# Second pass of a gated cross-attention kernel: the masks are written into the score banks by VectorE and ScalarE instead of by TensorE

## The chip, the cores and the metric

The kernel runs on one NeuronCore of one Trainium2 chip. The metric is the device time of one execution in microseconds (us), smaller is better. Engines: TensorE (PE, its weight loads PEld), VectorE (DVE), ScalarE (ACT), GpSimd (POOL) and SyncE (SP), which only issues DMAs here.

## The reference

```python
# x: (128, 128, 256); ctx_1024: (128, 128, 256); mask: (128, 128, 128) int32, per item [query, key]
# block 0: attention without weights (16 heads of 16), then an fp8 GEMM, each added to x through tanh(gate)
# block 1:
qh, kh, vh = (proj(q, Wq, bq), proj(k, Wk, bk), proj(v, Wv, bv))
scores = einsum('bhqd,bhkd->bhqk', qh, kh) / sqrt(16)
scores = where(mask[:, None] == 0, -1e9, scores)
attn = softmax(scores, axis=-1)
ctx = einsum('bhqk,bhkd->bqhd', attn, vh)
out = concat @ Wo.T + bo            # added to x through tanh(g_xattn[1])
# then a layer norm, an int8-like activation quantisation with one scale for the whole tensor, a ternary GEMM
```

There are 128 batch items, and each item is one tile of 128 queries by 128 keys by 256 features. The change concerns only the masked attention of block 1.

## The kernel before

X stays in SBUF for all 128 items. The program runs three passes over it: the first (`step_a`) is block 0, the second (`step_b`) is the attention of block 1 with the statistics of its last norm, the third (`step_c`) is the quantised GEMM. Every engine has its own written-out order; there is no scheduler. In the second pass a step i works on several items at once: `live(off)` says whether item i + off exists, the projections are those of item i+1, the maximum scores those of item i, the exponent scores those of item i-2, the normalising and output projection those of item i-3, and a norm's last part those of item i-7. Fori loops repeat eight written-out steps. Steps alternate between even and odd k; in even steps ScalarE makes two normalised inputs `xn`, in odd ones GpSimd works out the norm statistics of a pair.

Softmax takes its row maxima from one set of scores (queries on the partitions, `max_pair`, two PSUM banks, `bank_max`) and its exponentials from a second, transposed set (keys on the partitions, `exp_pair`, two banks, `bank_exp`). Each bank pair holds half of the 16 heads at a time, so a step fills each pair twice: `fill(0, ...)` and `fill(1, ...)`. A fill of the maximum pair is read by one VectorE reduction (`max_pair_of`, L787), one of the exponent pair by one ScalarE exponential (`exp_pair_of`, L553). `U` and `UM` are the projected queries and keys, `UM` with the even or the odd heads set to zero; GpSimd makes `UM` (L519, L521) and reports it with `m_made`.

In `fill`, the matmuls of a 32-partition row group r are L1044 (maximum) and L1051 (exponent); the two kinds use different row groups and run side by side. The mask is added by TensorE: L1035 writes the mask into the maximum banks through an identity ahead of the scores (2 matmuls of 512 columns), L1058 adds the transposed mask to the exponent banks behind them (2 more). L1039 writes the negated row maxima (`sh_T`), which VectorE splits into two bf16 parts (`sh`), TensorE transposes (L1157) and ScalarE copies out (L612).

The further orders that the change's steps meet:

- TensorE: fill 0, L1026 (attention output back), L1157, L1165 and L1173 (projections q, k and v), fill 1, L1068 (weighing with V, pair 1), L1192, wait for `m_made` and `xn_made`, L1206 (transposes of the next inputs), L1068 (pair 0), L1218 (output projection).
- ScalarE: L553 (exponential 1), L612, in even steps L557 twice (`xn`), L625 (`n2`, held in the tile `ff_y`), L630 (V), L553 (exponential 0), L638, L645, L547.
- GpSimd: in odd steps the statistics L485 to L502, L505, then wait for `n2_made`: L510 and L512 (gamma and beta on `n2`), then L519 and L521 (`UM`).
- VectorE: L886, norm statistics, L916, L787, L927 and L778, L934 (mask to bf16, 0 or -2^100), L941 (`U`), L787, L948 and L950 (`sh`).

Of the kernel before, what the change touches and what calls it, by code (L numbers as in the profile page):

```python
# [30 lines left out]
P = 128  # L31
# [24 lines left out]
def build(nc, x, ctx, mask, g_xattn, g_ffn, f8_kernel, in_scale, kernel_scale, f8_bias,  # L56
# [12 lines left out]
    with stack:  # L69
# [46 lines left out]
        sh_T = [sb(f"sh_T{n}", [P, 4 * P], BF16)[:, :] for n in range(2)]  # L116
# [109 lines left out]

        bv_made = sem("bv_made")
# [305 lines left out]
        def _(act):  # L533
# [70 lines left out]

            def step_b(i, k, live):
# [27 lines left out]
                if live(-2):  # L633
                    exp_pair_of(0)
                if live(-3):
# [3 lines left out]
                      .then_inc(cn_out, 1)  # L639
                if live(2):  # L640
# [31 lines left out]
        def _(vec):  # L672
# [205 lines left out]

            def step_b(i, k, live):
# [13 lines left out]
                if live(5):  # L893
                    n_bn = mine(v.bn_stats(st6_b[n][:, 0:6], xs(i + 5)))
                if odd and (live(5) or live(-5)) and (live(1) or live(-9)):
# [16 lines left out]
                if live(-8):  # L912
# [5 lines left out]
                    if live(-7 + 1):  # L918
# [3 lines left out]
                if live(0):  # L922
                    max_pair_of(0, k % 2).then_inc(max_read, 1)
                if live(-3):
                    vec.wait_ge(attn_back, 1)
                    vec.sem_inc(attn_back, -1)
                    mine(v.reciprocal(rden[:, :], bank_oh[:, :, DH]))  # L927
                    settle()
                    attn_normed().then_inc(attn_read, 1)
                if live(1):  # L930

                    vec.wait_ge(mask_in[(k + 1) % 2], 16)
                    vec.sem_inc(mask_in[(k + 1) % 2], -16)
                    n_m = mine(v.tensor_scalar(mask_b[(k + 1) % RING], mask_i[(k + 1) % 2], 0.0, MASKED,  # L934
                                               ALU.is_equal, ALU.mult))
                    vec.wait_ge(qk_proj, 1)
                    vec.sem_inc(qk_proj, -1)  # L937
                    settle(n_m)
                    if live(3):
                        vec.sem_inc(mask_used, 1)  # L940
                    v.tensor_tensor(U[(k + 1) % RING][:, :, :], bank_t[0][:, :].rearrange("p (c t) -> p c t", c=4),  # L941
# [328 lines left out]
```

## Time and profile before

| | before |
|---|---|
| median of 3 runs | 2464.26 us (2459.34 to 2464.36) |
| the profiled execution | 2460.99 us, its span 2459.2 us |
| mean granted TensorE clock | 0.978 |
| busy: PE, PEld | 2168.4 us (88%), 1537.5 us (63%) |
| busy: DVE, ACT, POOL | 1611.5 us (66%), 1430.5 us (58%), 1129.2 us (46%) |
| second pass | from about 892 to about 2345 us of the span |

Busy times are summed records of an engine, and a record can overlap the next one. In the rows of the timeline a line is one instruction or several of the same kind in a row ("x2"), with the start in us from the span's start and the duration in us; what stands in brackets is the idle time of the engine just before it and what ended it. `PEq L1149` is a wait of the TensorE's instruction queue at line 1149.

### The profile page before, as it was taken

To read this page: it belongs to the slowest core of one execution; us is meant where nothing else is said; L and a number is where in the kernel's file an instruction comes from. 1 tells how busy PE (TensorE), PEld (TensorE's weight loads), DVE (VectorE), ACT (ScalarE), POOL (GpSimd) and SP (SyncE) were. 2 spreads that over 40 slices of the span, in tenths; PEclk is the share of its full clock that TensorE was granted. 3 is DMA by queue.
4 is the path that set the end of the run, shared out by engine and by line. 5 is a ranking of instruction groups with operands and counts; after the bars stand their busy time and mean duration, and the time that the engine had idled before them with its cause. 6 is when DMAs were issued, how large, how long until landed. Compare 5 with 4: busy or idle time off the path is not lost. (4 is left out here: it accounts for less than half of the span.)

```text
span 2459.2 us, 74014 instructions
## 1 busy us (share of the span) xinstructions
PE 2168.4 (88%) x25884; PEld 1537.5 (63%) x25884; DVE 1611.5 (66%) x3702; ACT 1430.5 (58%) x2375; POOL 1129.2 (46%) x1905
## 2 busy tenths in 40 slices
PE   3888888888888859999999999999999999999957
PEld 2666666666666547667666766666666666666635
DVE  4888888888888845555555555555554555555569
ACT  1788787887877734444444444544544444544469
POOL 2666666666666633433343343434333433434320
PEclk6999999999999979999999999999999999999989
DMA  2111111111111000000000000000000000000025
GB/s 70 45 40 43 40 41 43 40 41 42 39 43 43 15 21 21 21 18 21 18 21 18 19 20 18 21 18 21 17 21 18 21 18 18 21 18 21 4 85 189
DMA packets 95564, 80.56 MB, mean 33 GB/s; under 512 B 11392, under 2 KB 95360, under 8 KB 95360
## 3 DMA queue, kind: packets, MB, share of 16 engines
q1 hardware_dynamic: 95360, 77.44, 10.4%
q8 instruction: 176, 2.88, 0.5%
q14 instruction: 28, 0.23, 0.0%
HBM read 60.63 MB, written 16.78 MB: 31 GB/s over the span
## 5 line engine op out<-in xcount | busy, mean ns | idle before, releaser
L553 ACT ACTIVATE probs<-bank_exp 128x1024 f32<-128x1024 f32 x512 | 523.8, 1023 | 679.0 <-ACTq L552 679.0
L787 DVE TENSOR_REDUCE a_nmax<-bank_max 128x8 f32<-128x1024 f32 x512 | 625.7, 1222 | 330.9 <-DVEq L786 326.2
L1044 PE MATMUL bank_max<-UM,U 32*128 32x256 f32 x4096 | 588.7, 405 | 4.6 <-PEq L1079 2.5
L1051 PE MATMUL bank_exp<-UM,U 32*128 32x256 f32 x4096 | 531.1, 377 | 0.0
L510 POOL TENSOR_TENSOR ff_y<-ff_y,gamma_bc 128x256 f32<-128x256 f32 x128 | 92.8, 725 | 804.8 <-POOLq L509 804.8
L1068 PE MATMUL bank_o<-probs,V 128*17 128x128 f32 x8192 | 324.2, 275 | 127.4 <-PEq L1064 126.9
L1051 PEld LDWEIGHTS bank_exp<-UM,U 32*128 32x128 f32 x4096 | 391.9, 185 | 0.6
L1068 PEld LDWEIGHTS bank_o<-probs,V 128*17 128x17 f32 x8192 | 187.7, 96 | 275.7 <-issue 275.3
L1044 PEld LDWEIGHTS bank_max<-UM,U 32*128 32x128 f32 x4096 | 354.3, 186 | 8.6 <-issue 7.9
L1165 PE MATMUL bank_t<-spare,wT 128*128 128x128 f32 x2048 | 259.1, 280 | 0.9 <-PEq L1162 0.9
L1165 PEld LDWEIGHTS bank_t<-spare,wT 128*128 128x128 f32 x2048 | 241.3, 194 | 1.6 <-issue 1.6
L886 DVE SCALAR_TENSOR_TENSOR X<-bank_m,gate,X 128x256 f32 (+1 forms) x128 | 61.9, 484 | 269.1 <-DVEq L885 269.1
L1039 PE MATMUL bank_exp<-sh_T,ones_b 32*128 32x512 bf16 x1024 | 199.7, 385 | 16.1 <-PEq L1115 11.3
L547 ACT ACTIVATE attn_T<-bank_o 128x512 f32<-128x512 f32 x256 | 152.9, 597 | 90.6 <-ACTq L546 90.4
L1035 PE MATMUL bank_max<-ff_qT,ident 128*128 128x512 bf16 x512 | 152.8, 380 | 34.0 <-PEq L1149 33.5
L941 DVE TENSOR_TENSOR U<-bank_t,bqk_T 128x512 f32<-128x512 f32 x128 | 88.5, 691 | 133.9 <-DVEq L937 133.9
L1026 PE MATMUL bank_o<-identf,attn_T 128*128 128x128 f32 x1024 | 162.9, 282 | 0.9 <-PEq L1024 0.9
L1026 PEld LDWEIGHTS bank_o<-identf,attn_T 128*128 128x128 f32 x1024 | 119.5, 142 | 69.3 <-issue 45.9
L1039 PEld LDWEIGHTS bank_exp<-sh_T,ones_b 32*128 32x128 bf16 x1024 | 50.4, 91 | 175.2 <-issue 151.4
L1058 PE MATMUL bank_exp<-ident,ff_qT 128*128 128x512 bf16 x512 | 157.1, 389 | 0.0
L472 POOL TENSOR_TENSOR spare<-spare 128x512 f32<-128x512 f32 x64 | 81.5, 1273 | 144.0 <-POOLq L471 87.0
L449 POOL TENSOR_SCALAR UM<-U,heads_eo 128x512 f32<-128x512 f32 x128 | 119.4, 933 | 59.9 <-POOLq L448 59.8
(163 smaller groups left out, 4151.6 us busy)
## 6 DMA issues: line engine op xcount, KB each, us to landing
ctx<-in_ctx SPq DMA_DIRECT2D x256, 128.0 KB, 2.1
X<-in_x SPq DMA_DIRECT2D x128, 128.0 KB, 2.1
out_y<-X SPq DMA_DIRECT2D x64, 256.0 KB, 2.1
ff_qq<-in_mask_BxSxS_ik SPq DMA_DIRECT2D x128, 64.0 KB, 1.8
X<-in_L_xattn_Wq SPq DMA_DIRECT2D x1, 256.0 KB, 2.7
X<-in_L_xattn_Wk SPq DMA_DIRECT2D x1, 256.0 KB, 3.1
X<-in_L_xattn_Wv SPq DMA_DIRECT2D x1, 256.0 KB, 3.8
X<-in_L_xattn_Wo SPq DMA_DIRECT2D x1, 256.0 KB, 4.2
```

What stands on the lines that cost most here:

```text
L449: mine(nc.gpsimd.tensor_scalar(UM[s][:, :, 0, :], U[s][:, :, :], heads_eo[:, 0:1], 0.0, ALU.mult, ALU.add))
L547: nc.scalar.activation(attn_T[:, :, :].rearrange("p g t -> p (g t)"), bank_o[:, :], ACT.Copy)\
L553: nc.scalar.activation(a_probs[n], exp_pair[:, :, :, :].rearrange("p i h t -> p (i h) t"), ACT.Exp, scale=SCALE).then_inc(probs_made, 1)
L787: return v.tensor_reduce(a_nmax[:, k2, n * H // 2:(n + 1) * H // 2], max_pair[:, :, :, :].rearrange("p i h t -> p (i h) t"), axis=AX.X, op ...
L1026: last = nc.tensor.transpose(bank_o[:, g * P:(g + 1) * P], attn_T[:, g, :], identf[:, :])
L1035: mm(max_pair[:, b, :, :], ident[:, :], mask_now.rearrange("p (o t) -> p o t", o=1) .broadcast_to([P, HG, P]), start=True, stop=False, ski ...
L1039: mm(exp_pair[:, r % 2, :, :], ones_b[32 * r:32 * r + 32, :], sh_T[ring][32 * r:32 * r + 32, :], start=True, stop=False, skip_group_check= ...
L1044: last = mm(max_pair[:, r % 2, 2 * c:2 * c + 2, :], U[now][32 * r:32 * r + 32, c, :], UM[now][32 * r:32 * r + 32, DC + c, :, :], start=not ...
L1051: last = mm(exp_pair[:, r % 2, 2 * c:2 * c + 2, :], U[before][32 * r:32 * r + 32, DC + c, :], UM[before][32 * r:32 * r + 32, c, :, :], sta ...
L1058: last = mm(exp_pair[:, b, :, :], mask_before, ident[:, :].rearrange("p (o t) -> p o t", o=1) .broadcast_to([P, HG, P]), start=False, stop ...
L1068: last = mm(bank_o[32 * j:32 * j + VW, (2 * c + n) * P:(2 * c + n + 1) * P], V[k4][:, 8 * c + 2 * r + e, :], a_probs[n][:, r % 2 * HG + 2 ...
L1165: last = mm(bank_t[0][:, n * P:(n + 1) * P], wT[n // DC][:, c, n % DC * P:(n % DC + 1) * P], in_T[(k + 1) % 2][:, n // DC * DC + c, :], st ...
```

## The change

TensorE no longer writes masks. VectorE copies the mask (`mask_b`, queries on the partitions) into both maximum banks, spread over 8 heads, directly after each maximum reduction (`seed_max`). ScalarE copies the transposed mask into both exponent banks in the same way after each exponential (`seed_exp`). All score matmuls and the shift now add to what is there (`start=False`). Once, at the start of the second pass, TensorE writes to all four banks so that later matmuls add. The transposed mask comes from a fifth transpose beside the four of `sh`, and the copy L612 takes five blocks instead of four. In `fill` the shift moves from the first to the last place. On VectorE, the reduction of fill 0 and what follows it move ahead of the norm's aggregates and L916.

```diff
+        sh_mask_T = [sb(f"sh_T{n}", [P, 5 * P], BF16)[:, :] for n in range(2)]
+        sh_T = [t[:, 0:4 * P] for t in sh_mask_T]
+        mask_T = [t[:, 4 * P:5 * P] for t in sh_mask_T]
...
         # scalar
+            def seed_exp(ring):
+                nc.scalar.activation(exp_pair[:, :, :, :].rearrange("p i h t -> p (i h) t"),
+                                     mask_T[ring].rearrange("p (o t) -> p o t", o=1).broadcast_to([P, H // 2, P]),
+                                     ACT.Copy).then_inc(exp_seeded, 1)
+            def exp_settled(n):
+                act.wait_ge(scores, 1)
+                act.sem_inc(scores, -1)
+                nc.scalar.activation(a_probs[n], exp_pair[:, :, :, :].rearrange("p i h t -> p (i h) t"), ACT.Exp,
+                                     scale=SCALE).then_inc(act_own, 1)
+            def probs_settled():
+                act.wait_ge(act_own, 1)
+                act.sem_inc(act_own, -1)
+                act.sem_inc(probs_made, 1)
...
                 if live(-2):
-                    exp_pair_of(1)
+                    exp_settled(1)
                 if live(-1):
                     act.wait_ge(shift_Td, 1)
                     act.sem_inc(shift_Td, -1)
-                    nc.scalar.activation(sh_T[(k + 1) % 2], bank_tb[1][:, 0:4 * P], ACT.Copy).then_inc(shift_out, 1)
+                    nc.scalar.activation(sh_mask_T[(k + 1) % 2], bank_tb[1][:, 0:5 * P], ACT.Copy).then_inc(shift_out, 1)
+                if live(-2):
+                    probs_settled()
+                    seed_exp(k % 2)
...
                 if live(-2):
-                    exp_pair_of(0)
+                    exp_settled(0)
                 if live(-3):
                     act.wait_ge(cn_T, 1)
...
+                if live(-1):
+                    if live(-2):
+                        probs_settled()
...
+                    seed_exp((k + 1) % 2)
...
         # vector
+            def seed_max(ring):
+                v.tensor_copy(max_pair[:, :, :, :].rearrange("p i h t -> p (i h) t"),
+                              mask_b[ring].rearrange("p (o t) -> p o t", o=1).broadcast_to([P, H // 2, P]))\
+                 .then_inc(max_seeded, 1)
...
+                if live(0):
+                    n_max = mine(max_pair_of(0, k % 2))
+                    settle(n_max)
+                    seed_max(k % RING)
...
                 if live(0):
                     n_max = mine(max_pair_of(1, k % 2))
                     settle(n_max)
-                    vec.sem_inc(max_read, 1)
+                if live(1):
+                    seed_max((k + 1) % RING)
...
         # tensor, in fill
-                if now is not None and masked:
-                    for b in range(2):
-                        mm(max_pair[:, b, :, :], ident[:, :], mask_now.rearrange("p (o t) -> p o t", o=1)
-                           .broadcast_to([P, HG, P]), start=True, stop=False, skip_group_check=True)
...
-                                      start=not masked, stop=True, skip_group_check=True)
+                                      start=not seeded, stop=True, skip_group_check=True)
...
-                if before is not None and masked:
-                    for b in range(2):
-                        last = mm(exp_pair[:, b, :, :], mask_before, ident[:, :].rearrange("p (o t) -> p o t", o=1)
-                                  .broadcast_to([P, HG, P]), start=False, stop=True, skip_group_check=True)
-                    last.then_inc(scores, 1)
+                if before is not None and seeded:
+                    add_shift(False).then_inc(scores, 1)
...
         # tensor, ahead of and in step_b
+            for b in bank_max + bank_exp:
+                last = mm(b, ident[:, :], ident[:, :].rearrange("p (o t) -> p o t", o=1).broadcast_to([P, HG, P]),
+                          start=True, stop=True, skip_group_check=True)
+            last.then_inc(primed, 2)
...
+                if live(0):
+                    pe.wait_ge(max_seeded, 1)
+                    pe.sem_inc(max_seeded, -1)
+                if live(-2):
+                    pe.wait_ge(exp_seeded, 1)
+                    pe.sem_inc(exp_seeded, -1)
+                fill(0, now, before, k % 2, True)
...
+                    nc.tensor.transpose(bank_tb[1][:, 4 * P:5 * P], mask_b[(k + 3) % RING], ident[:, :])\
+                      .then_inc(shift_Td, 1)
```

On ScalarE this is an even step of the second pass, from its first exponential to `V`, before (L553 the exponential, L612 the copy of the shift, L557 the two `xn`, L625 `n2`, L630 `V`):

```order
422 L553 ACTIVATE probs<-bank_exp 128x1024
423 L612 ACTIVATE sh_T<-bank_t 128x512
424 L557 ACTIVATE xn<-X,a_shift,a_rstd 128x256 x2
425 L625 ACTIVATE ff_y<-X,shift,rstd 128x256
426 L630 ACTIVATE V<-bank_m 128x16x16
```

And this is the same place now (L617 is `seed_exp`, which reads the mask's block of `sh_T`):

```order
455 L624 ACTIVATE probs<-bank_exp 128x1024
456 L640 ACTIVATE sh_T<-bank_t 128x640
457 L617 ACTIVATE bank_exp<-sh_T 128x1024
458 L564 ACTIVATE xn<-X,a_shift,a_rstd 128x256 x2
459 L656 ACTIVATE ff_y<-X,shift,rstd 128x256
460 L661 ACTIVATE V<-bank_m 128x16x16
```

A copy of 1024 elements per partition now stands between the shift's copy and the `xn` and `n2` instructions, and the shift's copy has 640 elements instead of 512.

On TensorE this is the stretch from the output projection L1218 over fill 0 to the projections L1165, before:

```order
932 L1218 MATMUL bank_m<-wT,ff_xy 128x256 x2
933 L1035 MATMUL bank_max<-ff_qT,ident 128x512 x2
934 L1039 MATMUL bank_exp<-sh_T,ones_b 128x512 x2
935 L1044 MATMUL bank_max<-UM,U 128x256 x2
936 L1051 MATMUL bank_exp<-UM,U 128x256 x2
937 L1044 MATMUL bank_max<-UM,U 128x256 x2
938 L1051 MATMUL bank_exp<-UM,U 128x256 x2
939 L1058 MATMUL bank_exp<-ident,ff_qT 128x512 x2
940 L1026 MATMUL bank_o<-identf,attn_T 128x128 x4
941 L1157 MATMUL bank_t<-ident,sh 128x128 x4
942 L1165 MATMUL bank_t<-spare,wT 128x128 x8
```

And the same stretch now (L1096 and L1103 are the scores, L1088 the shift, L1215 the mask's transpose):

```order
925 L1278 MATMUL bank_m<-wT,ff_xy 128x256 x2
926 L1096 MATMUL bank_max<-UM,U 128x256 x2
927 L1103 MATMUL bank_exp<-UM,U 128x256 x2
928 L1096 MATMUL bank_max<-UM,U 128x256 x2
929 L1103 MATMUL bank_exp<-UM,U 128x256 x2
930 L1088 MATMUL bank_exp<-sh_T,ones_b 128x512 x2
931 L1079 MATMUL bank_o<-identf,attn_T 128x128 x4
932 L1214 MATMUL bank_t<-ident,sh 128x128 x4
933 L1215 MATMUL bank_t<-ident,ff_qT 128x128
934 L1222 MATMUL bank_t<-spare,wT 128x128 x8
```

Four matmuls of 512 columns have left the fill, one transpose has come, and the shift stands last in the fill.

## Rows read from the trace of the kernel before

**Rows 1.** The page's busy shares and its 40 slices of the span.

```profile
PE 2168.4 (88%) x25884; PEld 1537.5 (63%) x25884; DVE 1611.5 (66%) x3702; ACT 1430.5 (58%) x2375; POOL 1129.2 (46%) x1905
...
PE   3888888888888859999999999999999999999957
...
PEclk6999999999999979999999999999999999999989
```

**Rows 2.** Windows: busy us (instructions) of each engine, granted clock, DMA share, GB/s.

```profile
350.00:850.00 500.00, 414.32 (x6585) 303.76 (x6574) 442.46 (x1012) 399.34 (x625) 335.50 (x508) 1.00 0.13 39
...
912.00:2310.00 1398.00, 1354.12 (x14214) 945.50 (x14213) 748.54 (x1731) 658.38 (x1117) 542.17 (x982) 0.99 0.07 19
```

**Rows 3.** Timeline of TensorE, one even step, then one odd step.

```profile
1499.15 0.48 PE L1044 MATMUL bank_max<-UM,U 32*128 32x256 f32 x2
...
1507.53 0.41 PE L1206 MATMUL bank_t<-identf,xn 128*128 128x128 f32 x2
...
1509.62 0.59 PE L1035 MATMUL bank_max<-ff_qT,ident 128*128 128x512 bf16 x2
1510.15 0.48 PE L1044 MATMUL bank_max<-UM,U 32*128 32x256 f32 x2
...
1511.33 0.61 PE L1058 MATMUL bank_exp<-ident,ff_qT 128*128 128x512 bf16 x2
1511.78 0.60 PE L1026 MATMUL bank_o<-identf,attn_T 128*128 128x128 f32 x4
1512.21 0.39 PE L1157 MATMUL bank_t<-ident,sh 128*128 128x128 bf16 x4
1512.44 2.00 PE L1165 MATMUL bank_t<-spare,wT 128*128 128x128 f32 x16
...
1515.14 0.59 PE L1035 MATMUL bank_max<-ff_qT,ident 128*128 128x512 bf16 x2
...
1516.85 0.61 PE L1058 MATMUL bank_exp<-ident,ff_qT 128*128 128x512 bf16 x2
1517.39 0.63 PE L1068 MATMUL bank_o<-probs,V 128*17 128x128 f32 x16
...
1518.22 0.38 PE L1206 MATMUL bank_t<-identf,xn 128*128 128x128 f32 x2
...
1520.82 0.48 PE L1044 MATMUL bank_max<-UM,U 32*128 32x256 f32 x2
```

**Rows 4.** Timeline of ScalarE, the same even step's chain, then the odd step's.

```profile
1501.07 1.02 ACT L553 ACTIVATE probs<-bank_exp 128x1024 f32<-128x1024 f32 x1 [2.59 <-ACTq L552]
1501.99 0.59 ACT L612 ACTIVATE sh_T<-bank_t 128x512 bf16<-128x512 bf16 x1
1502.46 1.09 ACT L557 ACTIVATE xn<-X,a_shift,a_rstd 128x256 f32 x2
1503.45 0.60 ACT L625 ACTIVATE ff_y<-X,shift,rstd 128x256 f32 x1
...
1513.46 0.60 ACT L625 ACTIVATE ff_y<-X,shift,rstd 128x256 f32 x1
```

**Rows 5.** Timeline of GpSimd, the second UM of the even and of the odd step.

```profile
1506.39 0.69 POOL L521 TENSOR_SCALAR UM<-U,heads_eo 128x512 f32<-128x512 f32 x1
...
1516.41 0.69 POOL L521 TENSOR_SCALAR UM<-U,heads_eo 128x512 f32<-128x512 f32 x1
```

**Rows 6.** Timeline of VectorE from the same two steps.

```profile
1505.96 1.23 DVE L787 TENSOR_REDUCE a_nmax<-bank_max 128x8 f32<-128x1024 f32 x1 [1.57 <-DVEq L786]
1507.34 0.20 DVE L948 CAST sh<-a_nmax 128x16 bf16<-128x16 f32 x1
...
1510.04 0.48 DVE L886 SCALAR_TENSOR_TENSOR X<-bank_m,gate,X 128x256 f32 x1 [2.23 <-DVEq L885]
```

**Rows 7.** Timeline of the first pass: a `UM` operation beside VectorE's L828.

```profile
609.15 1.22 POOL L449 TENSOR_SCALAR UM<-U,heads_eo 128x512 f32<-128x512 f32 x1 [0.62 <-POOLq L448]
...
609.24 0.66 DVE L828 TENSOR_TENSOR ff_qq<-spare 128x512 bf16<-128x512 f32 x1
```

More of the change, by code:

```diff
@@ L225, in build @@
         in_out = sem("in_out")
+        primed = sem("primed")
+        max_seeded = sem("max_seeded")
+        exp_seeded = sem("exp_seeded")
+        mask_T_made = sem("mask_T_made")
+        act_own = sem("act_own")
         bv_made = sem("bv_made")
@@ L603, in _ @@
             act.wait_ge(pass_ends[0], 5)
+            act.wait_ge(primed, 1)
+            act.sem_inc(primed, -1)
+            def seed_exp(ring):
[11 more added lines that the diff above has]
+                act.sem_inc(probs_made, 1)
             def step_b(i, k, live):
@@ L1027, in attn_transpose, with fill, add_shift @@
                 last.then_inc(attn_back, 1)
[L1029 to L1031 removed]
+            def fill(n, now, before, ring, seeded=False):
                 lo, hi = 2 * n, 2 * (1 - n)
[L1033 to L1040 removed]
+                def add_shift(start):
+                    for r in (hi, hi + 1):
+                        last = mm(exp_pair[:, r % 2, :, :], ones_b[32 * r:32 * r + 32, :],
+                                  sh_T[ring][32 * r:32 * r + 32, :], start=start, stop=False, skip_group_check=True)
+                    return last
+                if before is not None and not seeded:
+                    add_shift(True)
                 for c in range(DC):
@@ L1145, in step_b @@
                 before = (k + 2) % RING if live(-2) else None
-                masks = (mask_b[k % RING] if live(0) else None, mask_b[(k + 2) % RING] if live(-2) else None)
-                if live(-1):
-                    pe.wait_ge(max_read, 1)
-                    pe.sem_inc(max_read, -1)
-                fill(0, now, before, k % 2, *masks)
+                if live(0):
+                    pe.wait_ge(max_seeded, 1)
[4 more added lines that the diff above has]
+                fill(0, now, before, k % 2, True)
                 if live(-3):
@@ L1176, in step_b @@
                 if live(0):
-                    pe.wait_ge(max_read, 1)
-                    pe.sem_inc(max_read, -1)
+                    pe.wait_ge(max_seeded, 1)
+                    pe.sem_inc(max_seeded, -1)
                 if live(-2):
-                    pe.wait_ge(probs_made, 1)
-                fill(1, now, before, k % 2, *masks)
+                    pe.wait_ge(exp_seeded, 1)
+                    pe.sem_inc(exp_seeded, -1)
+                fill(1, now, before, k % 2, True)
                 if live(-1):
@@ L1184, in step_b @@
                     pe.sem_inc(shift_out, -1)
+                    if not live(-2):
+                        pe.sem_inc(mask_T_made, 1)
                 if live(-3):
```

61 lines of the change are left out of this document (29 added, 32 removed).

## The prediction

> **What bounds the kernel now.** I read the page first. TensorE is 88% busy, and the slices after the fourteenth stand at 9 in a row [rows 1]. The windows say it closer: in the second pass TensorE is busy 1354.1 of 1398 us (97%), VectorE 54%, ScalarE 47%, GpSimd 39%, at a granted clock of 0.99 [rows 2]. That speaks for TensorE as the bound, and for a change that takes matmuls away. But 97% says only that it rarely stands still now, not what stands right behind it. So I read the timeline of two steps, engine by engine.
>
> A step, from the first L1044 of one fill 0 to the next, takes 11.00 us where k is even (1499.15 to 1510.15) and 10.67 us where it is odd (1510.15 to 1520.82) [rows 3]. TensorE's work is the same in both. The odd step is TensorE's own length. The even one is 0.33 us longer because of a chain that goes through three other engines. Counted from the step's first L1044: exponential 1 starts on ScalarE at +1.92, then come L612, two L557, and L625 (`n2`) at +4.30 [rows 4]; GpSimd puts gamma and beta on `n2` and only then makes `UM`, whose second half ends at 1507.08 [rows 5]; L1206, which waits for that through `m_made`, starts at 1507.53, which is +8.38 [rows 3]. So from GpSimd's end to TensorE's start 0.45 us go by, and from the start of `n2` to L1206 4.08 us. In the odd step the chain has no L557: `n2` starts at +3.31, `UM` ends at 1517.10, so L1206 could start at 1517.55, and starts at 1518.22, +8.07 [rows 3 to 5]. There the chain has 0.67 us to spare. This is the point of my forecast: behind TensorE stands a chain of nearly the same length, and the change shortens one and lengthens the other.
>
> **What the change takes from TensorE.** The two mask matmuls ahead of the maximum scores move the first L1044 back by 0.53 us (L1035 at 1509.62 to L1044 at 1510.15) [rows 3]. The exponent masks take 0.45 us in fill 0 (1511.33 to 1511.78, where full weights follow them) and 0.54 in fill 1 (1516.85 to 1517.39, where narrow ones follow) [rows 3]. So I take some 0.44 for two such matmuls, and the 0.10 left over in the first and the third of these for the change of weight shape, which stays. Together 2 x 0.43 + 0.45 + 0.44 = 1.75 us a step. Added: a fifth transpose, 0.23 / 4 = 0.06 us (1512.21 to 1512.44) [rows 3]. Moving the shift inside a fill costs nothing or one half slot of about 0.1, since row groups stream side by side. TensorE alone would then need 10.67 - 1.69 = 8.98 us a step.
>
> **What it adds to the chain.** The shift is now the last thing in the fill, and exponential 1 waits for it. Before, the exponent group of a fill filled 1.18 us (1510.15 to 1511.33) and L1058 came on top; the exponential starts 0.74 us after the first of the L1058 pair (1500.33 for the even step by the same spacing, to 1501.07) [rows 3, 4]. Without the pair it starts at about +1.45, between +1.39 (the row groups start together) and +1.50 (half a slot later). L612 follows 0.92 us behind, +2.37. It had 0.47 to the next start; with 128 elements more at (1.02 - 0.59) / 512 = 0.84 ns each [rows 4] it has 0.58. At +2.95 stands the new instruction, ScalarE's seed.
>
> No row shows a ScalarE write to PSUM. The nearest is L553, as many elements from PSUM to SBUF: 1.02 us long, 0.92 to the next start [rows 4]. From below I bound the spacing by 0.84 ns x 1024 = 0.86 us (the elements alone), from above by 1.25 (0.92 and the 0.33 that a starved start could add, the difference of the two kinds of step here). I take 0.92, as the function costs nothing visible and count and width are equal. The ScalarE page of the Trainium skill (ScalarE: Activation LUTs, What ACT_TABLE_LOAD costs) gives 186 ns + 0.833 ns an element for an activation with immediate operands, and back-to-back overlap of some 93 ns. By it the seed would take 1.04 us and have 0.95 to the next start, against 0.92 from the row, which over 126 steps would be 4 us more; the trace agrees with the slope, 0.84 ns.
>
> In the **even** step `xn` starts at +3.87, `n2` 0.99 us later (1502.46 to 1503.45) at +4.86 [rows 4], L1206 4.08 later at +8.94. From L1206 to the next L1044 were 2.62 us; the mask's 0.43 is gone, 2.19 stay: 11.13 us, against 11.00. In the **odd** step `n2` starts at +3.87, and `UM` ends 3.64 later (1513.46 to 1517.10) [rows 4, 5], L1206 starts 0.45 behind it at +7.96, and 2.60 - 0.43 = 2.17 later the next fill: 10.13 us, against 10.67. A pair of steps takes 21.26 instead of 21.67 us, 0.41 less. 126 of the 128 items have both fills with everything alive, so 63 pairs give 26 us. TensorE, for all that is taken from it, stands still at L1206 for over 1.5 us a step. What was 1.69 a step becomes 0.2.
>
> **Where the seeds of VectorE stand.** No row shows a VectorE write of this size to PSUM; the reduction of as many elements takes 1.22 us [rows 6]. From below half of it, 0.6, from above a quarter more, 1.5. L886 starts at about +0.4 (0.11 ahead of L1044, and the masks' 0.53 no longer lie between) [rows 3, 6], two bn_stats follow, the reduction starts at about +1.5, the seed 0.15 after its end (the gap in front of L948) [rows 6] at +2.9, ends at +4.1 and is seen at some +4.25. Fill 1 comes at 4.99 - 0.45 + 0.06 + 0.10 = +4.7 (1510.15 to 1515.14) [rows 3]. So it is hidden with 0.45 us to spare, and at 0.6 more so; at 1.5 us 0.17 are left. What pays if that cover is gone is fill 1, but L1206 waits for `m_made` anyway, so up to 1.5 us of it would cost nothing either. The second seed has until the next fill 0, over 1.5 us. ScalarE's first seed ends at +3.97, also before fill 1; its second follows exponential 0 and L638 and lies in TensorE's new standstill. `probs_made` for the second L1068 comes later by the ScalarE queue's extra wait, some 0.15 us, but L1206 is later by more. `U` (L941) moves from +4.55 to about +4.9, and `UM` doesn't want it before +6.1.
>
> The ends of the pass have steps without a maximum fill, where the exponential's chain alone counts; four such steps with a seed each give back about 4 us. The priming is four matmuls in a stretch in which TensorE waits for its first input. Sum: -26 + 4 = -22 us. Against the profiled execution's 2460.99 that is 2439; the runs' median is 2464.26, three us above it, so I say 2442.
>
> **Rivals.**
> 1. *TensorE stays the bound*, and the 1.69 us a step come out nearly whole: 63 pairs of 21.67 - 17.96 = 3.71 us are 234 us, 2230 us. For it speaks the 97% [rows 2]; against it that L1206 is plainly tied to `m_made` in the even step, where it starts 0.45 us after `UM` [rows 3, 5]. It holds only if `n2` could start 1.2 us earlier than I work out.
> 2. *Slower: a VectorE seed blocks GpSimd's `UM`*. In the first pass a `UM` operation takes 1.22 us instead of 0.69 when VectorE's L828 runs beside it [rows 5, 7]. In the even step the second seed (+7.5 to +8.7) lies beside the second `UM` (+7.8 to +8.5). If it costs the same 0.53 there, the pair gains nothing: -0.41 + 0.53 = +0.12, 63 pairs are 8 us, with the 4 of the ends 2476. If the first seed meets GpSimd too, 2510. It decides from a delay of 0.41 us a pair. L828 reads two SBUF tensors, the seed one. By the Trainium skill (SBUF — State Buffer, SBUF: two separate sides) the port pair that VectorE and GpSimd share is an exclusive lock, and only a VectorE instruction with two SBUF inputs or in a two-port mode blocks GpSimd, and its VectorE page (VectorE: DVE Perf Modes, Why PSUM operands drop a tier) excludes that mode with a PSUM operand. By that the seeds block nothing and the time is my 2442; the row of the first pass agrees in that its blocker has two SBUF inputs.
> 3. *Slower: ScalarE's seed costs more than an exponential.* It lies in the chain in every step, so each 0.1 us is 12.6 us. The gain is gone at a spacing of 0.92 + 0.18 = 1.10 us; at my upper bound of 1.25 the time is 2442 + 0.33 x 126 = 2484.
> 4. *No change*: the terms of the chain are off by 0.2 us a step, as rounding of the fill's end (0.1) and the copy L612 (0.1) can do together: 2464.
>
> TensorE's clock: it stood at 1.00, the 2.4 GHz level, in the first pass, where TensorE was busy 414 of 500 us [rows 2]; it will now be busy about as much, so I expect no change.
>
> **How the numbers follow.** My case 0.53; rival 1 0.05; rivals 2 and 3 together 0.29; rival 4 0.13. Two executions differ by up to 5 us here (2459.34 to 2464.36), so 0.2% is about what can be told from no change. My case's own range goes from 2417 (seed spacing 0.86, exponential at +1.39, both some 0.1 us a step) to 2459. The range goes on to the slower cases, 2484, and leaves out rival 1 and the worst of rival 2. Faster: 0.53 + 0.05 = 0.58; same 0.13; slower 0.29.
>
> **What would show it.** In the profile of after, TensorE's busy share in the second pass falls from 97% to about 83%, and the wait in front of its L1206 becomes the largest of its waits, with some 1.6 us a step. Even steps take about 11.1 us and odd ones 10.1. ScalarE's seed stands between the shift's copy and `xn`, about 1.02 us long. GpSimd's `UM` keeps 0.69 us; 1.22 there would be rival 2. If TensorE waits instead at a score matmul for `max_seeded` or `exp_seeded`, my hidden terms were wrong, and if it doesn't wait at all, rival 1 holds.

## Result and profile after

| | before | after |
|---|---|---|
| median | 2461.8 us (2458.25 to 2464.36) | 2513.23 us (2511.3 to 2519.27) |
| the profiled execution | 2460.99 us | 2511.3 us, its span 2509.3 us |
| mean granted TensorE clock | 0.978 | 0.939 |

The ratio is 1.0213, with a 95% interval of 1.0195 to 1.0232: the kernel became 2.1% slower. 2442 was forecast.

The page of after (busy time, share, instructions; then TensorE and its clock in 40 slices):

```profile
PE 2069.2 (82%) x24992; PEld 1498.8 (60%) x24992; DVE 1895.0 (76%) x3958; ACT 1680.0 (67%) x2631; POOL 1130.1 (45%) x1905
PE   4888888888888769888888888888888888888857
PEclk7999999999999979999998998989989989999979
```

The nines in TensorE's row became eights, as forecast. New is the row below it: where it read 9 throughout the second pass [rows 1], several slices now read 8. The same two stretches as in [rows 2] (us; busy of PE, PEld, DVE, ACT and POOL, with their instructions; granted clock; DMA share; GB/s):

```profile
350.00:850.00 500.00, 414.19 (x6582) 303.77 (x6578) 442.69 (x1013) 399.46 (x625) 336.27 (x507) 1.00 0.14 39
912.00:2310.00 1398.00, 1212.26 (x12955) 876.40 (x12953) 999.18 (x1932) 874.49 (x1327) 527.05 (x957) 0.93 0.07 19
```

The first pass is what it was. In the second, TensorE's busy time fell by 142 us, and the granted clock from 0.99 to 0.93.

An even step of after on TensorE, shortened, to be read beside [rows 3]:

```profile
1610.81 0.48 PE L1096 MATMUL bank_max<-UM,U 32*128 32x256 f32 x2
...
1612.10 0.66 PE L1079 MATMUL bank_o<-identf,attn_T 128*128 128x128 f32 x4
...
1615.67 0.48 PE L1096 MATMUL bank_max<-UM,U 32*128 32x256 f32 x2
...
1619.83 0.41 PE L1266 MATMUL bank_t<-identf,xn 128*128 128x128 f32 x2 [1.87 <-PEq L1263]
...
1620.94 1.13 PE L1278 MATMUL bank_m<-wT,ff_xy 128*128 128x256 f32 x4
1622.01 0.48 PE L1096 MATMUL bank_max<-UM,U 32*128 32x256 f32 x2
```

L1096 is the former L1044 (maximum scores), L1266 the former L1206 (transposes that wait for `m_made`), L1278 the former L1218. The step takes 11.20 us, the odd one behind it 10.23. TensorE stands still for 1.87 us ahead of L1266; its own work is 11.20 - 1.87 = 9.33 us at most (the idle time is counted from the modelled end of the matmul before).

ScalarE and GpSimd in the same step, to be read beside [rows 4, 5] (L624 is exponential, L640 the copy of shift and mask, L617 the seed, L564 `xn`, L656 `n2`; L526 and L528 the two halves of `UM`):

```profile
1612.30 1.02 ACT L624 ACTIVATE probs<-bank_exp 128x1024 f32<-128x1024 f32 x1 [1.73 <-ACTq L623]
1613.22 0.70 ACT L640 ACTIVATE sh_T<-bank_t 128x640 bf16<-128x640 bf16 x1
1613.80 1.04 ACT L617 ACTIVATE bank_exp<-sh_T 128x1024 f32<-128x1024 bf16 x1
1614.75 1.08 ACT L564 ACTIVATE xn<-X,a_shift,a_rstd 128x256 f32 x2
1615.73 0.59 ACT L656 ACTIVATE ff_y<-X,shift,rstd 128x256 f32 x1
```

```profile
1618.01 0.70 POOL L526 TENSOR_SCALAR UM<-U,heads_eo 128x512 f32<-128x512 f32 x1
1618.68 0.70 POOL L528 TENSOR_SCALAR UM<-U,heads_eo 128x512 f32<-128x512 f32 x1
```

VectorE, reduction and seed for each of the two halves:

```profile
1612.21 1.21 DVE L827 TENSOR_REDUCE a_nmax<-bank_max 128x8 f32<-128x1024 f32 x1
1613.45 1.23 DVE L924 CAST bank_max<-ff_qT 128x1024 f32<-128x1024 bf16 x1
...
1616.96 1.22 DVE L827 TENSOR_REDUCE a_nmax<-bank_max 128x8 f32<-128x1024 f32 x1 [0.24 <-DVEq L826]
1618.22 1.23 DVE L924 CAST bank_max<-ff_qT 128x1024 f32<-128x1024 bf16 x1
```

So the chain is the forecast one, link by link: exponential 1 at +1.49, seed at +2.99, `n2` at +4.92, `UM` ready at +8.57, L1266 at +9.02.

But that step is a good one. From the first to the last of 121 steps the mean is 11.52 us, where (11.20 + 10.23) / 2 would be 10.72. A part of that is in before too, since every eighth step is longer at the end of a loop body: there the mean is 11.20 and (11.00 + 10.67) / 2 is 10.84. Here is where the rest comes from, a few steps earlier (windows of 2 us, columns as above):

```profile
1592.00:1594.00 2.00, 2.00 (x29) 1.17 (x32) 1.61 (x7) 1.48 (x4) 0.61 (x1) 1.00 0.10 29
1594.00:1596.00 2.00, 0.84 (x18) 0.39 (x10) 1.97 (x2) 1.96 (x3) 1.92 (x4) 1.00 0.22 70
1596.00:1598.00 2.00, 1.20 (x20) 0.78 (x20) 0.71 (x3) 0.66 (x2) 1.63 (x5) 0.91 0.00 0
1598.00:1600.00 2.00, 2.00 (x8) 1.18 (x4) 0.00 (x0) 0.82 (x2) 1.13 (x4) 0.50 0.00 0
1600.00:1602.00 2.00, 2.00 (x20) 1.31 (x20) 1.29 (x4) 0.00 (x0) 0.00 (x0) 0.73 0.03 8
1602.00:1604.00 2.00, 2.00 (x21) 1.99 (x21) 1.97 (x2) 1.94 (x3) 0.00 (x0) 1.00 0.00 0
```

The timeline of TensorE at the fall:

```profile
1596.80 0.41 PE L1266 MATMUL bank_t<-identf,xn 128*128 128x128 f32 x2 [1.96 <-PEq L1263]
...
1598.13 2.08 PE L1278 MATMUL bank_m<-wT,ff_xy 128*128 128x256 f32 x4
```

TensorE stands still for 1.96 us ahead of L1266, resumes, and soon after its granted clock is at 0.50 (the 1.2 GHz level) for about 3 us. The four matmuls of L1278 take 2.08 us there and 1.13 at 1.00. Read in windows of 1 us from 920 to 2300 us of the span, the clock's shortfall adds up to 184 us at half clock in 38 falls, against 20 us in 6 falls before. (In both kernels the pass's end, behind 2300 us, lies outside this count.) In before too each fall has a standstill ahead of it, at the end of a loop body of eight steps:

```profile
1348.00:1350.00 2.00, 0.55 (x3) 0.14 (x1) 1.20 (x5) 0.24 (x1) 0.59 (x1) 1.00 0.05 8
1350.00:1352.00 2.00, 0.49 (x2) 0.13 (x2) 0.60 (x3) 0.00 (x0) 0.00 (x0) 0.96 0.03 8
1352.00:1354.00 2.00, 2.00 (x19) 1.60 (x18) 0.00 (x0) 0.00 (x0) 0.00 (x0) 0.50 0.00 0
```

### The profile page after: what moved, and what is told of

Same layout as the page of the kernel before. It is cut to its first block and busy times, and to the rows that moved or that the text cites. A ratio compares the mean times of both kernels' runs of the same rounds, so it can differ in the third digit from the quotient of the medians.

```text
span 2509.3 us, 73386 instructions
## 1 busy us (share of the span) xinstructions
PE 2069.2 (82%) x24992; PEld 1498.8 (60%) x24992; DVE 1895.0 (76%) x3958; ACT 1680.0 (67%) x2631; POOL 1130.1 (45%) x1905
## 5 line engine op out<-in xcount | busy, mean ns | idle before, releaser
L827 DVE TENSOR_REDUCE a_nmax<-bank_max 128x8 f32<-128x1024 f32 x512 | 625.7, 1222 | 178.9 <-DVEq L826 173.9
L1096 PE MATMUL bank_max<-UM,U 32*128 32x256 f32 x4096 | 609.3, 416 | 35.1 <-PEq L1206 27.4
L1103 PE MATMUL bank_exp<-UM,U 32*128 32x256 f32 x4096 | 580.6, 402 | 3.9 <-PEq L1238 3.9
L624 ACT ACTIVATE probs<-bank_exp 128x1024 f32<-128x1024 f32 x256 | 262.2, 1024 | 397.7 <-ACTq L623 397.7
L1096 PEld LDWEIGHTS bank_max<-UM,U 32*128 32x128 f32 x4096 | 368.0, 193 | 140.8 <-issue 131.9
L1103 PEld LDWEIGHTS bank_exp<-UM,U 32*128 32x128 f32 x4096 | 386.8, 192 | 5.6 <-issue 5.1
L924 DVE CAST bank_max<-ff_qT 128x1024 f32<-128x1024 bf16 x256 | 314.4, 1228 | 8.8
L560 ACT ACTIVATE probs<-bank_exp 128x1024 f32<-128x1024 f32 x256 | 262.0, 1024 | 83.2 <-ACTq L559 83.2
L617 ACT ACTIVATE bank_exp<-sh_T 128x1024 f32<-128x1024 bf16 x256 | 263.9, 1031 | 0.6 <-ACTq L630 0.4
L1222 PEld LDWEIGHTS bank_t<-spare,wT 128*128 128x128 f32 x2048 | 252.7, 201 | 1.6 <-issue 1.6
L1088 PE MATMUL bank_exp<-sh_T,ones_b 32*128 32x512 bf16 x1024 | 202.5, 389 | 14.8 <-PEq L1165 11.3
L1266 PE MATMUL bank_t<-identf,xn 128*128 128x128 f32 x256 | 53.3, 291 | 168.7 <-PEq L1263 168.5
L1278 PE MATMUL bank_m<-wT,ff_xy 128*128 128x256 f32 x512 | 176.2, 475 | 0.7 <-PEq L1276 0.7
L1079 PE MATMUL bank_o<-identf,attn_T 128*128 128x128 f32 x1024 | 173.8, 294 | 0.9 <-PEq L1077 0.9
L564 ACT ACTIVATE xn<-X,a_shift,a_rstd 128x256 f32 (+1 forms) x256 | 139.0, 596 | 13.1 <-ACTq L646 7.0
```

What stands on the lines that cost most here:

```text
L560: nc.scalar.activation(a_probs[n], exp_pair[:, :, :, :].rearrange("p i h t -> p (i h) t"), ACT.Exp, scale=SCALE).then_inc(probs_made, 1)
L617: nc.scalar.activation(exp_pair[:, :, :, :].rearrange("p i h t -> p (i h) t"), mask_T[ring].rearrange("p (o t) -> p o t", o=1).broadcast_t ...
L624: nc.scalar.activation(a_probs[n], exp_pair[:, :, :, :].rearrange("p i h t -> p (i h) t"), ACT.Exp, scale=SCALE).then_inc(act_own, 1)
L827: return v.tensor_reduce(a_nmax[:, k2, n * H // 2:(n + 1) * H // 2], max_pair[:, :, :, :].rearrange("p i h t -> p (i h) t"), axis=AX.X, op ...
L924: v.tensor_copy(max_pair[:, :, :, :].rearrange("p i h t -> p (i h) t"), mask_b[ring].rearrange("p (o t) -> p o t", o=1).broadcast_to([P, H ...
L1079: last = nc.tensor.transpose(bank_o[:, g * P:(g + 1) * P], attn_T[:, g, :], identf[:, :])
```

## Experiments

Two theories. **Clock:** the chain alone would have given the forecast gain or most of it; what made the kernel slower is that TensorE, standing still at L1266 in every step, loses its clock. **Chain:** the seed of ScalarE lengthens the path to `n2` by more than I priced, and the clock costs little. Ratios below are to the kernel before, on the same chip, with their 95% interval; "low" is the time at half clock, counted as above from 920 to 2300 us. The faster kernels are in the pass's end, or past it, before 2300 us; where that matters it is said. The filler matmuls of some kernels are work that nobody reads. All kernels compute the whole result.

**1. Fillers in the standstill.** After, with 16 small bf16 matmuls in even and 8 in odd steps ahead of the wait for `m_made`, into an unused part of `bank_m` (the wait `v_out` moves ahead of them):

```diff
+                if live(1) and live(-3):
+                    for _ in range(8 if k % 2 else 16):
+                        mm(bank_m[:, D:2 * D], ident[:, :], f8_w[:, 0, :], start=True, stop=True)
                 if live(1):
                     pe.wait_ge(m_made, 1)
```

> Built on the changed kernel. In front of TensorE's wait for m_made stand matmuls that no one reads (128x128 weights, 256 columns, bf16): 16 in even steps, 8 in odd ones, which fill the standstill that the trace shows there (1.87 us and 0.91 us). The chain through ScalarE and GpSimd keeps its length. Theory 1 (the loss is TensorE's clock, which falls after standstills): the granted clock of the second pass rises from 0.93 to 0.98 or more, the steps take 11.2 and 10.2 us throughout but for the loop ends, and the time falls by some 55 us, to about 2455. Theory 2 (the loss is the longer chain itself, and the clock only follows an idle engine): the time stays at 2510, whatever the clock does. Theory 3 (the seeds disturb other engines): 2510 too, or more.

Measured 2513.72 us, ratio 1.019 [1.0173, 1.0207]: no gain. Within a loop body every step was now at full clock, 11.21 and 10.23 us, as the clock theory says. But the step behind each loop end took 14.3 to 15.9 us, with 104 us low in 14 falls: at the loop ends TensorE still stood still (33.4 us in 15 waits, and 17.6 us in 13 more inside the fill that follows, the gap that is shown at experiment 5), and at half clock the fillers are themselves late. The total alone would have spoken for the wrong theory. The steps decide.

**2. `n2` ahead of the seed and of `xn`** on ScalarE, after otherwise unchanged:

```diff
-                if live(-2):
-                    probs_settled()
-                    seed_exp(k % 2)
-                if not odd and live(2):
-                    ...
                 if live(-7):
                     ...
                     nc.scalar.activation(n2[k % 2], xs(i - 7), ACT.Identity, bias=col(shift4, i - 7),
                                          scale=col(rstd4, i - 7)).then_inc(n2_made, 1)
+                if live(-2):
+                    probs_settled()
+                    seed_exp(k % 2)
+                if not odd and live(2):
+                    ...
```

> The changed kernel with another order on ScalarE: n2 directly behind the shift's copy, then the seed, then the two xn. The seed and the xn leave the chain to UM. Theory 1 and the account of the chain: L1266 can start some 2 us earlier in the even step and 1 us earlier in the odd one, steps of 9.4 us, almost no standstill, clock 0.98 or more, time about 2280. Theory 2 says the same of the chain but nothing of the clock. Theory 3 (the seeds disturb other engines, VectorE is now too full): VectorE needs some 8 us a step with the seeds, it becomes the bound, steps of 10 us or more, 2350 or higher.

Measured 2353.24 us, 0.954 [0.9524, 0.9556]. The chain is shorter, but the time missed the expected 2280 by 73 us. Steps of 9.66 us, 0.3 above the 9.33 of TensorE's own work. The bound stands one link on: GpSimd now waits for `U` ahead of L526, in 123 steps. First the waits of after, then of this kernel, from 912 to 2340 us (engine, tile and line, what it waited for; us in total, times, longest):

```profile
PE bank_t L1266 <- PEq L1263: 161.7, 117, 2.0
```

```profile
POOL UM L526 <- POOLq L523: 89.5, 123, 7.5
PE bank_t L1266 <- PEq L1263: 42.1, 113, 1.7
```

The standstill shrinks from 1.4 to 0.4 us a step. Low time goes from 184 to 96 us, and 44 of the 96 lie in the pass's end, behind 2209 us, which after reaches only behind 2340 us and which is low there too (48 us from 2340 to 2440); so the count without the ends goes from 184 to 51 us. One reordered instruction is worth 160 us, by steps and by clock together: the gain of the change had been locked behind it.

**3 and 4. Half of the change each.** First VectorE's seeds alone, with the exponent masks still by TensorE (its edit, in part, against after); then ScalarE's seeds alone, with the maximum masks by TensorE and VectorE's order of before.

```diff
-                if live(-2):
-                    probs_settled()
-                    seed_exp(k % 2)
...
-                    add_shift(False).then_inc(scores, 1)
+                    for b in range(2):
+                        last = mm(exp_pair[:, b, :, :], mask_before, ...
```

> Half of the change: VectorE's seeds and its new order, the maximum masks gone from TensorE; the exponent masks stay on TensorE and ScalarE is as before. Theory 1: the chain keeps its length, TensorE loses 0.43 us a fill; even steps about 10.6 us (0.7 us of standstill), odd ones about 9.8 to 10.2, so the time falls by 60 to 80 us, to about 2390, unless the clock falls there too. Theory 3 (VectorE's seeds harm): at or above 2462.

> The other half: ScalarE's seeds, the exponent masks gone from TensorE; the maximum masks stay on TensorE and VectorE is as before. Theory 1: the chain is longer by the seed, a pair of steps takes 22.1 instead of 21.7 us at full clock, that is 28 us, and standstills of 1.7 and 0.7 us a step make the clock fall, so 2490 without and up to 2560 with the fallen clock. Theory 3 (VectorE's seeds harm): this half is the harmless one, 2462 or less.

VectorE's half: 2396.11 us, 0.9715 [0.9698, 0.9733], steps of 10.58 and 9.96 us, 52 us low in 9 falls (18 of them in the pass's end). ScalarE's half: 2506.23 us, 1.0153 [1.013, 1.0176], steps of 11.64 and 10.67. So the seed of VectorE is hidden and pays, and the seed of ScalarE in the chain costs more than its matmuls did. Both fit the working of the chain. The second speaks against half of the clock theory: its TensorE waited for `m_made` 1.6 us at the longest, 114.5 us in all, and was low for 17 us only. It is slower by its steps, not by the clock (its wait from 912 to 2340 us, and its windows):

```profile
PE bank_t L1257 <- PEq L1254: 114.5, 119, 1.6
```

```profile
912.00:2200.00 1288.00, 1150.61 (x12386) 810.35 (x12385) 708.06 (x1556) 798.60 (x1222) 489.35 (x887) 0.99 0.07 19
```

After has 1115.90 of 1288 us busy in the same stretch, only 35 less, at 0.93. Standstills as such don't bring the clock down; which do is not told by these runs.

The two halves don't add up: -2.85% and +1.53% would be -1.3%, and together they cost +2.1%, some 85 us more. The lengths of good steps nearly add up (a pair would take 20.54 + 22.31 - 21.67 = 21.18 us and takes 21.43, 16 us over 63 pairs). The rest has the size of what the clock is found to cost below; that it is the clock's is argued, not measured by these two runs.

**5 and 6. Fillers at the loop end too, and there alone.** Ten bf16 matmuls of 512 columns behind the last step of each loop body:

```diff
+                if not isinstance(i, int) and k == 0:
+                    for _ in range(10):
+                        mm(bank_t[1][:, :], ident[:, :], ident[:, :].rearrange("p (o t) -> p o t", o=1)
+                           .broadcast_to([P, HG, P]), start=True, stop=True, skip_group_check=True)
```

> The fillers of the first experiment, and ten more matmuls of 512 columns behind the last step of each loop body, queued ahead of TensorE's jump back, so that they run while its queue jumps. The first experiment left the steps inside the loops at 11.21 and 10.23 us but made the step behind each loop end 14.3 to 15.9 us long, at half clock. Theory 1 (the clock falls at a standstill, wherever it is): now no standstill is left, the granted clock of the second pass is 0.99 or more, the step behind a loop end takes 10.2 us, eight steps take about 88.2 us instead of 93, and the time is 2440 to 2450. Theory 2 (the fillers shift the fall of the clock elsewhere, and a chip that does this work has it somewhere): the time stays at 2513.

> The changed kernel with only the ten matmuls behind each loop body, none in front of the wait for m_made. Theory 1 with both kinds of standstill at work: the step behind the loop end is short again, but slow steps stay in the middle of the loops, so the time lies between, 2475 to 2500. If the loop ends alone bring the clock down: 2445, the clock at 0.99. If they have no part: 2513.

Both kinds: 2502.43 us, 1.0147 [1.0131, 1.0162], 41 us low. That missed by 60 us. Within the loop body all was as expected; behind 13 loop ends there is a second standstill, inside the first fill (24.0 us in all), which waits for nothing that the trace shows, and 12 times the clock fell behind it. Experiment 1 has it too:

```profile
1545.98 0.37 PE L1096 MATMUL bank_max<-UM,U 32*128 32x256 f32 x1 [1.58 <-issue]
```

The fillers at the loop end alone: 2499.88 us, 1.0124 [1.0106, 1.0142], 109 us low in 33 falls, now in the middle of loop bodies. As expected: the two places are separate.

**7 and 8. The loop-end fillers on before, and on experiment 2.** The edit is that of 5.

> The kernel before with the same ten matmuls behind each loop body. In its trace 6 of 14 loop ends are followed by a step of 12.3 instead of 10.67 us. Theory 1: these six go, 10 us in all, so 0.996 of the kernel before, and no further gain, since its clock is 1.00 elsewhere. Theory 2: no difference.

> The second experiment's kernel (n2 ahead of the seed and of xn) with the ten matmuls behind each loop body. There the step behind a loop end takes 10.93 instead of 9.66 us, 13 times, and a loop end 13.1. Theory 1: 17 to 20 us less than the second experiment, about 0.946 of the kernel before. Theory 2: 0.954 as in the second experiment.

Before with them: 2457.67 us, 0.9967 [0.9955, 0.9979], nothing low; the six long steps (five of 12.1 to 12.3 us, one of 11.7) are gone. Experiment 2 with them: 2337.98 us, 0.9482 [0.9467, 0.9496]; the step behind a loop end takes 9.71 us instead of 10.93, and up to 2186 us, where the pass's end begins, it is low for 3 us only. By the ratios it gained 14 us, where 17 to 20 were expected. In both, unread work in a standstill makes the kernel faster, which the clock explains and nothing else that I know of in the traces does.

**9. The same cover from fewer instructions.** Experiment 5 with fp32 fillers, which stream longer each: 3 and 1 of 256 columns in the steps, 2 of 512 columns behind the loop body (the edit in the steps against experiment 5; the wait `v_out` stands ahead of them as in 1).

```diff
-                    for _ in range(8 if k % 2 else 16):
-                        mm(bank_m[:, D:2 * D], ident[:, :], f8_w[:, 0, :], start=True, stop=True)
+                    for _ in range(1 if k % 2 else 3):
+                        mm(bank_m[:, D:2 * D], identf[:, :], wvT[:, 0, :], start=True, stop=True)
```

> The changed kernel with fewer, longer fillers: in front of the wait for m_made three fp32 matmuls of 256 columns in even steps and one in odd ones, and two fp32 matmuls of 512 columns behind each loop body. The fifth experiment's many short ones left a second gap of 1.6 us behind each loop end, in which TensorE waited for nothing that the trace shows, and the clock fell right behind it. Theory 1 with that gap as the effect of a longer program: without it eight steps take 88 to 89 us, the clock of the second pass stays above 0.98 and the time is 2440 to 2460. If the gap stays, 2490 to 2500.

Measured 2446.08 us, 0.9926 [0.9911, 0.994]. This is the run that settles the question: the change, with unread matmuls added and one wait of TensorE earlier, is faster than before. First the windows of after, then of this kernel, and its L1272 (the former L1266):

```profile
912.00:2200.00 1288.00, 1115.90 (x11927) 806.57 (x11925) 920.88 (x1779) 805.22 (x1222) 488.06 (x887) 0.93 0.07 19
```

```profile
912.00:2200.00 1288.00, 1215.88 (x12968) 885.92 (x12967) 960.19 (x1857) 837.76 (x1274) 507.36 (x924) 1.00 0.07 20
```

```profile
1614.41 0.41 PE L1272 MATMUL bank_t<-identf,xn 128*128 128x128 f32 x2 [0.57 <-PEq L1269]
```

The clock is 1.00, the steps take 11.19 and 10.22 us, as the good ones of after, and 4% more instructions of VectorE (1857 against 1779) and ScalarE (1274 against 1222) fit into the same 1288 us. L1272 still waits for the chain. The second standstill behind the loop ends is gone. The two kernels that have it show 76362 and 76642 instructions in their traces (experiments 1 and 5), all others at most 74490 (this one); so the number of instructions in the loop body may bring it, but no run isolates that.

**10. The order alone, on before.** `n2` ahead of `xn` in even steps, no seeds.

> The kernel before with n2 ahead of the two xn in even steps, nothing else. By the chain as the prediction reads it the even steps fall from 11.00 to 10.67 us, TensorE's own length, 63 times 0.33 us or 20 us, 0.992 of the kernel before. If TensorE had been the only bound before: no difference.

Measured 2449.89 us, 0.9947 [0.9933, 0.996]: 13 us gained where 20 were expected. All steps but those at the loop ends take 10.66 us, TensorE's own, as the prediction read the chain; 8 loop ends instead of 6 are followed by a fall of the clock (31 us low instead of 20), which takes back some of it. So of experiment 2's gain only 0.5% is the order's own; the rest is the change, once the order lets it through.

**11. A standstill without any seed.** Before, with GpSimd's first `UM` operation done three times over:

```diff
-                    mine(nc.gpsimd.tensor_scalar(UM[s][:, :, 0, :], U[s][:, :, :], heads_eo[:, 0:1], 0.0,
-                                                 ALU.mult, ALU.add))
+                    for _ in range(3):
+                        mine(nc.gpsimd.tensor_scalar(UM[s][:, :, 0, :], U[s][:, :, :], heads_eo[:, 0:1], 0.0,
+                                                     ALU.mult, ALU.add))
+                        settle()
```

> The kernel before, masks on TensorE and no seeds, with GpSimd's first UM instruction done three times, which makes the chain 1.48 us longer. It gives TensorE standstills of 1.8 us in even and 0.8 us in odd steps, as long as those of the changed kernel. The steps come to 12.5 and 11.5 us at full clock, 146 us in all or 2608. Theory 1 (standstills bring the clock down, whoever causes them): slow steps as in the changed kernel, 100 us or more of the second pass at half clock, and 2640 to 2670. Theory 3 (the seeds have a part in it): the clock stays as in the kernel before, and the time at 2608.

Measured 2691.26 us, 1.093 [1.0914, 1.0946], with 122 us low in 34 falls; steps of 12.7 and 11.7 us at full clock (0.2 longer than I expected), 13.2 to 14.3 where it fell. TensorE's wait and its windows:

```profile
1580.29 0.41 PE L1208 MATMUL bank_t<-identf,xn 128*128 128x128 f32 x2 [1.85 <-PEq L1205]
```

```profile
912.00:2200.00 1288.00, 1125.39 (x11235) 770.95 (x11235) 644.08 (x1368) 519.91 (x881) 569.42 (x980) 0.96 0.06 17
```

A kernel with TensorE's masks and none of the change's writes loses its clock in the same way when the same wait grows to the same length. It is not the seeds that do it.

**12. What both kernels leave.** Experiment 8, and on VectorE mask and `U` ahead of normalising the attention, since GpSimd now waited for `U`:

```diff
-                if live(-3):
-                    vec.wait_ge(attn_back, 1)
-                    ...
-                    attn_normed().then_inc(attn_read, 1)
                 if live(1):
                     ...
                     v.tensor_tensor(U[(k + 1) % RING][:, :, :], ...
+                if live(-3):
+                    vec.wait_ge(attn_back, 1)
+                    ...
+                    attn_normed().then_inc(attn_read, 1)
```

> The eighth experiment's kernel (n2 first, fillers behind the loop bodies) and on VectorE the mask and U ahead of the normalising of the attention output. In the second experiment GpSimd waits 0.35 us a step for U, and TensorE 0.33 us for UM. Theory of the chain: both waits go, the steps come to TensorE's own 9.33 us instead of 9.66, 2300 us or 0.933 of the kernel before. If the normalising, now later, is wanted earlier than that, fill 1's weighing waits and the time stays at 2338.

Measured 2298.54 us, 0.9321 [0.9308, 0.9333], steps of 9.35 us, as expected. Its windows (the 0.98 comes from the pass's end behind 2153 us, where it is low for 58 us; up to 2150 us the clock is 0.99):

```profile
912.00:2200.00 1288.00, 1244.49 (x13793) 897.72 (x13792) 1051.80 (x2031) 908.42 (x1401) 569.17 (x1025) 0.98 0.07 21
```

It is the fastest of all, 6.8% below before and, by the medians, 8.5% below after. The 9.35 us are not quite TensorE's own length. L1266 still starts 0.46 us behind the end of `UM`:

```profile
1508.11 0.69 POOL L528 TENSOR_SCALAR UM<-U,heads_eo 128x512 f32<-128x512 f32 x1
```

```profile
1508.80 0.44 PE L1252 MATMUL bank_t<-identf,attn 128*128 128x128 f32 x2
1509.26 0.41 PE L1266 MATMUL bank_t<-identf,xn 128*128 128x128 f32 x2
```

It also starts 0.46 us behind L1252. In the odd step of before, where `UM` was ready earlier, L1206 followed 0.27 us behind its L1192 (to 1518.22 in [rows 3]):

```profile
1517.95 0.44 PE L1192 MATMUL bank_t<-identf,attn 128*128 128x128 f32 x2
```

By that difference TensorE's own length would be some 9.16 us; that is an estimate from these rows, which no run reached.

## Why the prediction was wrong

- **The step that failed** is "TensorE's clock: it stood at 1.00 [...] in the first pass, where TensorE was busy 414 of 500 us [rows 2]; it will now be busy about as much, so I expect no change". The busy share came out (87% in the second pass, 83% in the first), and the clock did not: 0.93 in the one, 1.00 in the other. A share over hundreds of us does not decide the clock. It fell behind standstills of nearly 2 us. The evidence stood in the trace before: 0.99, not 1.00, in [rows 2], with falls behind 6 of the loop ends. I read 0.99 as "full". The Trainium skill (TensorE: Matmul & The Clock Gate, A second HAM failure mode: psum-queue depth-cycling) tells of a kernel in which frequent short standstills between groups of matmuls make the clock swing between its two levels; after and experiment 11 agree with it, and experiment 4, with a wait in as many steps (119 against 117), was low for 17 us only.
- **What it cost:** after has 184 us at half clock and experiment 9 has 6. The 178 us between them hold at most 89 us of lost work. From the ratios the two are (1.0213 - 0.9926) x 2461.8 = 71 us apart.
- **The chain** was right in mechanism and too small in size. Predicted 11.13 and 10.13 us, measured 11.20 and 10.23. Exponential 1 came 0.04 later than +1.45, the seed took 0.95 to the next start instead of 0.92; the fill with the shift took 1.29 us (1610.81 to 1612.10), the upper of my two values for it. 0.17 a pair in 63 pairs are 11 us, so -22 becomes -11. The cleanest measure of it is the change with the clock held in both kernels, experiments 9 and 7: (0.9926 - 0.9967) x 2461.8 = -10 us. That the two are so close is partly luck, since the -11 still has the forecast 4 us for the ends of the pass. From the last fill 1 with maximum scores to the last output projection after takes 31.84 us and before 23.57, 8 us more. There the steps have no projections between the fills, and three times TensorE stands still for some 1.95 us at its wait for `exp_seeded` ahead of fill 1 (L1238; TensorE's timeline of after, the second of the three):

```profile
2372.31 1.97 PE L1103 MATMUL bank_exp<-UM,U 32*128 32x256 f32 x8 [1.95 <-PEq L1238]
```

- **ScalarE's seed** is 1.04 us long with 0.95 to the next start (1613.80 to 1614.75). By the Trainium skill (ScalarE: Activation LUTs, What ACT_TABLE_LOAD costs) the estimate worked out ahead was 1.04 and 0.95; the trace agrees, and a bound near the page's figure would have been better than the exponential's row. Rival 3 is refuted.
- **VectorE's seeds** are hidden, by more than I said: the first ends at +3.87 (forecast +4.1), fill 1 starts at +4.86 (+4.7). Inside the loop bodies no step waits for `max_seeded`. Experiment 3 shows that they pay.
- **Rival 2** is refuted: the second seed (1618.22 to 1619.45) lies beside the second `UM` half, which takes 0.70 us.
- **Rival 1** is refuted for the change as it stands: L1266 waits 1.87 and 0.91 us a step, 1.4 in the mean; forecast was 1.6. Its size was too large as well. Of the 1.69 us a step that TensorE was to save, 1.32 came out, in experiment 12, when the chain was rearranged (10.67 to 9.35 us). Twice 0.11 us of the rest is the shift inside the fill (1.29 us against 1.18), and 0.19 the later L1266 shown there.
- The range (2415 to 2484) missed since no term in it was for the clock. -22 became -11 by the chain, and +71 came on top, less what falls before already cost (8 us by experiment 7): -11 + 71 - 8 = +52, and measured is +51 (the -11 is worked from step lengths, the other two are measured). The sum closes because the -11 is close to the -10 of experiments 9 and 7: with -10 in its place it would close by arithmetic alone, and proves nothing more.

**Open:** which standstills bring the clock down. The good step above has a wait of 1.87 us at L1266, and its L1278 takes 1.13 us. In the last step ahead of the next loop end, the same wait of the same length is followed by a fall (TensorE's timeline of after):

```profile
1641.26 0.41 PE L1266 MATMUL bank_t<-identf,xn 128*128 128x128 f32 x2 [1.87 <-PEq L1263]
...
1642.67 2.07 PE L1278 MATMUL bank_m<-wT,ff_xy 128*128 128x256 f32 x4
1646.21 0.80 PE L1096 MATMUL bank_max<-UM,U 32*128 32x256 f32 x2 [1.47 <-PEq L1206]
```

So one wait's length does not decide it, nor does the share over the pass; experiment 4, with waits up to 1.6 us, hardly falls at all. Whether the sum of several waits decides it, and which sum, was not settled.

## What to carry to other kernels

Where a change takes work from a busy engine, look for what stands next behind it in each step, and put the instruction that the chain needs ahead of the new one: here the same change was worth +2.1% or -4.6% by the place of `n2` alone. Where it leaves TensorE standing still in every step, read the granted clock in short windows behind the standstills that the kernel already has, not as a mean, and price a fall at what rows at half clock show. A total that does not move can hide two effects; compare step by step.

## What the runs showed of the hardware

- A granted clock of 0.50 for 3 us and more (184 us in 38 falls) behind standstills of some 2 us, at 87% busy over the pass, in after; and 1.00 at 83% busy from 350 to 850 us of the first pass.
- At the end of each loop body TensorE waits some 2 us ahead of its first scores (27.4 us in 15 waits in after), and in the two kernels with the most instructions (experiments 1 and 5) there was a second gap inside the fill that follows, 1.58 us in the one shown, which no semaphore explains.
- Unread matmuls made three kernels faster: before by 0.3%, experiment 2 by 0.6%, after by 2.8%.
- Both ScalarE and VectorE write PSUM banks to which matmuls then add, at 1.04 and 1.23 us for 128x1024 elements.
